# Gated cross attention and a routed expert layer: packed loop counts, a respread closing, smaller GpSimd pieces, and another table of steps

## The reference

```python
h = layernorm(x)
q, k, v = h @ Wq, ctx @ Wk, ctx @ Wv              # 8 heads of 64
o = softmax(q @ k.T / 8) @ v                      # per head, 512 x 1024 scores
x = x + tanh(g_xattn) * (o @ Wo + bo)
h = layernorm(x)
probs = softmax(h @ router.T)                     # 8 experts, each token takes its 2 best
# each expert keeps its CAPACITY (1280) heaviest tokens; kept weights are renormalised per token
y[e] = (h[e] @ W1[e].T * silu(h[e] @ Wg[e].T)) @ W2[e].T   # width 1024 inside
x = x + tanh(g_ffn) * sum over the kept experts of weight * y[e]
```

## Time and profile before

| | |
|---|---|
| median of 3 runs | 1721.95 us (1721.58 to 1724.79) |
| profiled execution | 1727.69 us, its span 1726.0 us |
| TensorE busy | 1642.6 us (95%), clock 0.996 |
| VectorE busy | 1270.0 us (74%) |
| ScalarE, GpSimd busy | 1050.0 us (61%), 671.9 us (39%) |
| chain that ended last | PE 76%, DVE 11%, issue 4%, POOL 3%, ACT 3% |

### The profile page before, as it was taken

The page is one execution under the profiler, slowest core; times in us unless marked ns, Lnnn a source line. Parts: engine busy times, 40 slices in busy tenths (PEclk is TensorE's granted clock), DMA queues, the critical chain, the costliest instruction groups (busy, mean ns, idle before and its releaser), DMA issues.

```text
span 1726.0 us, 33535 instructions
## 1 busy us (share of the span) xinstructions
PE 1642.6 (95%) x12454; PEld 1494.2 (87%) x12454; DVE 1270.0 (74%) x2595; ACT 1050.0 (61%) x2179; POOL 671.9 (39%) x615
## 2 busy tenths in 40 slices
PE   6999999999999999999999998999999999999997
PEld 4788878887888887888888886889999999999997
DVE  6887888888888888888888878676565556547443
ACT  5776766766767666766676766535454455546443
POOL 3342444444345345245345334423343422232322
PEclk9999999999999999999999999999999999999999
DMA  4200220121121021031030022314423421341212
GB/s 126 124 25 1 85 77 26 64 86 38 35 107 45 17 121 50 13 124 51 13 124 32 20 120 85 135 44 106 114 41 108 111 34 39 97 113 28 38 32 28
DMA packets 60555, 115.49 MB, mean 67 GB/s; under 512 B 6616, under 2 KB 48480, under 8 KB 59776
## 3 DMA queue, kind: packets, MB, share of 16 engines
q1 hardware_dynamic: 37104, 79.24, 13.0%
q0 software_dynamic: 15392, 18.66, 5.9%
q10 hardware_dynamic: 7920, 15.73, 2.6%
HBM read 90.27 MB, written 57.42 MB: 86 GB/s over the span
## 4 chain that ended last, share of the span: by engine, by line
PE 76%; DVE 11%; issue 4%; POOL 3%; ACT 3%; DMA 1%; POOLq 0%; DVEq 0%; SPq 0%; ACTq 0%
PE ring L1207 11%; PE turned L1101 11%; PE ffn L1064 10%; PE ffn L1066 10%; PE ffn L1065 10%; PE scores L1089 9%; DVE neg_max L1888 5%; PE ring L1064 4%; PE ring L1066 3%; PE ring L1065 3%; DVE pt_l L1665 2%; PE ring L1173 1%; PE ring L1175 1%; POOL lists L855 1%; POOL probs L889 1%
## 5 line engine op out<-in xcount | busy, mean ns | idle before, releaser
L889 POOL TENSOR_SCALAR probs<-probs,row_rec 128x1024 f32<-128x1024 f32 x254 | 282.2, 1123 | 478.6 <-DVE row_rec L1991 466.9
L1429 ACT ACTIVATE pt_h<-turned 128x512 fp32r<-128x512 f32 x512 | 279.5, 602 | 209.7 <-PE turned L1101 209.2
L1665 DVE TENSOR_TENSOR pt_l<-turned,pt_h 128x512 fp32r<-128x512 f32 x512 | 331.0, 680 | 7.2 <-ACT pt_h L1429 6.8
L1888 DVE TENSOR_REDUCE neg_max<-scores 128x1 f32<-128x1024 f32 x256 | 301.5, 1218 | 35.7 <-PE scores L1089 35.6
L1101 PE MATMUL turned<-ident,probs 128*128 128x128 f32 x2048 | 281.9, 279 | 30.3 <-DVE pt_l L1665 23.3
L1101 PEld LDWEIGHTS turned<-ident,probs 128*128 128x128 f32 x2048 | 224.2, 141 | 98.4 <-issue 69.9
L1485 ACT ACTIVATE probs<-scores,neg_max 128x1024 f32<-128x1024 f32 x256 | 285.3, 1117 | 14.9 <-DVE neg_max L1888 14.8
L1207 PE MATMUL ring<-pt_h,v_hl 128*128 128x256 f32 x1024 | 261.4, 293 | 0.2
L1207 PE MATMUL ring<-pt_l,v_hl 128*128 128x256 f32 x1024 | 250.9, 283 | 0.0
L2256 DVE TENSOR_TENSOR act_f<-ffn,silu 128x256 f32<-128x256 f32 (+1 forms) x232 | 108.4, 467 | 130.7 <-ACT silu L1599 123.3
L1207 PEld LDWEIGHTS ring<-pt_h,v_hl 128*128 128x128 f32 x1024 | 195.7, 191 | 4.0 <-issue 1.9
(11 more groups left out here) (258 smaller groups left out, 3905.4 us busy)
## 6 DMA issues: line engine op xcount, KB each, us to landing
lists<-pads SPq DMA_DIRECT2D x8, 4160.0 KB
w_raw<-w_t ACTq DMA_DIRECT2D x10, 1024.0 KB, 8.3
e_rows<-lists SPq DMA_DIRECT2D x26, 390.0 KB
ctx_raw<-ctx_t SPq DMA_DIRECT2D x15, 512.0 KB, 3.8
wg_raw<-wg_t ACTq DMA_DIRECT2D x5, 1024.0 KB, 7.8
x_in<-x SPq DMA_DIRECT2D x8, 512.0 KB, 4.0
x_sum<-x SPq DMA_DIRECT2D x8, 512.0 KB, 4.0
out<-x_sum SPq DMA_DIRECT2D x8, 512.0 KB, 2.9
```

The costliest lines, as they stand in the source:

```text
L889: nc.gpsimd.tensor_scalar(probs[:, k, :], probs[:, k, :], row_rec[:, k:k + 1], 1.0, ALU.mult, ALU.mult).then_inc(scaled, 1)
L1429: return nc.scalar.activation(dst, src, ACT.Copy)
L1665: return nc.vector.tensor_tensor(dst, src, hi_part.bitcast(F32), ALU.subtract)
L1888: nc.vector.tensor_reduce(neg_max[:, k:k + 1], scores[:, n % 2, :].rearrange("p (a c) -> p a c", a=2), AX.XY, ALU.max, negate=True).then_i ...
```

## The change

1. **Table of steps.** `JOBS` has the same jobs at other steps. The last batch keeps its table, written out. A new table `LOW_EARLY` says for the other batches how many of the two `low_turned` of an even step stand between its two maxima (1 or 2) instead of behind them. SP waits for job q(0,0) instead of v(0,0) before it loads the next x.
2. **GpSimd's pieces.** `split_ctx` makes its copy in two instructions of 128x512 instead of one of 128x1024, and its subtraction in four of 128x256.
3. **Closing.** `chain` has steps 4 to 16 spread otherwise. The table of counts is made in two parts (slots 0 and 1), the search's parts come one slot later or more, and the last one (normalising the kept weights) falls in part c = 1 of the first chunk behind the closing (`search(FC + 1)`).
4. **Loop counts.** VectorE packs each expert's two counts into 6 bits and four experts into a number. TensorE reads two such numbers once, in front of the search loop, and takes the counts of experts 1 to 7 out with shifts and remainders in registers; `before` is carried from expert to expert. The other engines still read theirs.

```diff
 JOBS = {
     0: [("w", 1, 0), ("k", 1, 0)],
     2: [("w", 1, 1)],
     3: [("k", 1, 1)],
     4: [("w", 1, 2), ("q", 1, 0)],
     6: [("w", 1, 3)],
-    7: [("v", 1, 0)],
-    8: [("v", 1, 1), ("k", 2, 0)],
-    10: [("k", 2, 1)],
-    12: [("h", 0, 0), ("v", 1, 2)],
-    13: [("q", 2, 0)],
-    14: [("v", 1, 3)],
-    15: [("q", 3, 0)],
-    16: [("h", 1, 0), ("w", 0, 0)],
-    18: [("w", 0, 1)],
-    19: [("l", 0, 0)],
-    20: [("k", 3, 0), ("w", 0, 2)],
-    21: [("k", 3, 1)],
-    22: [("x", 0, 0), ("x", 1, 0)],
-    23: [("v", 0, 0)],
-    24: [("w", 0, 3), ("k", 0, 0)],
-    27: [("q", 0, 0), ("r", 0, 0)],
-    28: [("k", 0, 1), ("v", 0, 1)],
-    29: [("v", 0, 2)],
+    7: [("k", 2, 0)],
+    8: [("v", 1, 0)],
+    9: [("v", 1, 1)],
+    10: [("q", 2, 0)],
+    12: [("k", 2, 1)],
+    13: [("h", 0, 0)],
+    14: [("v", 1, 2)],
+    15: [("w", 0, 0)],
+    16: [("w", 0, 1), ("k", 3, 0)],
+    17: [("v", 1, 3)],
+    18: [("h", 1, 0)],
+    19: [("w", 0, 2), ("l", 0, 0)],
+    20: [("k", 3, 1), ("q", 3, 0)],
+    22: [("x", 0, 0)],
+    23: [("w", 0, 3), ("x", 1, 0)],
+    24: [("v", 0, 0), ("k", 0, 0)],
+    26: [("k", 0, 1)],
+    27: [("v", 0, 1), ("r", 0, 0)],
+    28: [("v", 0, 2), ("q", 0, 0)],
     30: [("v", 0, 3)],
 }
+LOW_EARLY = {0: 2, 2: 2, 4: 1, 8: 2, 12: 2, 14: 1, 16: 1, 18: 1, 22: 1, 24: 1, 28: 1, 30: 1}
...
-                (0, 0): (4, 5, 6, 7, 8), (0, 1): (9, 10), (0, 2): (11,), (0, 4): (12, 13), (0, 5): (14, 15),
-                (0, 6): (16,), (0, 7): (17, 18), (1, 0): (19,), (1, 1): (20,), (1, 2): (21,), (1, 4): (22, 23),
+                (0, 0): (4, 5, 6, 7), (0, 1): (8, 9), (0, 2): (10, 11), (0, 5): (12, 13), (0, 6): (14, 15),
+                (0, 7): (16,), (1, 0): (17, 18), (1, 1): (19, 20), (1, 2): (21,), (1, 4): (22, 23),
...
-                nc.gpsimd.tensor_scalar(ctx_h[:, :, part], ctx_raw[:, :, :], 1.0, 1.0,
-                                        ALU.mult, ALU.mult).then_inc(ctx_hi, 1)
+                for kc in range(KC):
+                    last = nc.gpsimd.tensor_scalar(ctx_h[:, kc, part], ctx_raw[:, kc, :], 1.0, 1.0,
+                                                   ALU.mult, ALU.mult)
+                last.then_inc(ctx_hi, 1)
...
-                nc.gpsimd.tensor_tensor(ctx_l[:, :, part], ctx_raw[:, :, :],
-                                        ctx_h[:, :, part].bitcast(F32), ALU.subtract)\
-                    .then_inc(ctx_split, 1)
+                for kc in range(KC):
+                    for keys in range(2):
+                        raw = slice(keys * (M // 4), (keys + 1) * (M // 4))
+                        cols = slice(part.start + raw.start, part.start + raw.stop)
+                        last = nc.gpsimd.tensor_tensor(ctx_l[:, kc, cols], ctx_raw[:, kc, raw],
+                                                       ctx_h[:, kc, cols].bitcast(F32), ALU.subtract)
+                last.then_inc(ctx_split, 1)
...
@@ TensorE @@
-                part = {1: 1, 4: 3, 6: 4, 8: 5}.get(slot)
+                part = {1: 1, 5: 3, 6: 4, 9: 5}.get(slot)
...
+                    for k in range(2):
+                        loops.append(pe.value_load(table[0:1, 3, 3 + k:4 + k], min_val=1,
+                                                   max_val=(1 << FIELD * PER_WORD) - 1))
...
-                wides = pe.value_load(table[0:1, 4, ds(e, 1)], min_val=1, max_val=2)
-                chunks = pe.value_load(table[0:1, 0, ds(e, 1)], min_val=1, max_val=T // CHUNK)
-                before = pe.value_load(table[0:1, 1, ds(e, 1)], min_val=0, max_val=MOST_CHUNKS)
+                both = loops[(e - 1) // PER_WORD] >> FIELD * ((e - 1) % PER_WORD)
+                wides = pe.snap(both % 4)
+                chunks = pe.snap((both >> 2) % (1 << FIELD - 2))
...
@@ VectorE @@
+                    done = 0
+                    if body.own and (body.prev or u >= 2):
+                        done = (LAST_EARLY if body is LAST else LOW_EARLY).get(u, 0)
...
-                        if lows:
-                            low_turned(b, u - 2, 0)
-                            low_turned(b, u - 2, 1)
+                        for j in range(done):
+                            low_turned(b, u - 2, j)
...
-                part = {0: 0, 1: 1, 3: 2, 4: 3, 6: 4, 8: 6}.get(slot)
+                part = {0: 0, 1: 7, 2: 1, 3: 2, 4: 3, 8: 4, 9: 6}.get(slot)
...
+                    own(nc.vector.scalar_tensor_tensor(table_f[:, 7, :], table_f[:, 0, :], 4.0,
+                                                       table_f[:, 4, :], ALU.mult, ALU.add))
+                    v.wait_ge(search_seq, 24)
+                    v.wait_ge(powers, PER_WORD)
+                    own(nc.vector.tensor_tensor(table_f[:, 7, 1:E], table_f[:, 7, 1:E], table_f[:, 8, 1:E], ALU.mult))
+                    v.wait_ge(search_seq, 25)
+                    own(nc.vector.reduce_sum(table_f[:, 2, 2:3], table_f[:, 7, 1:1 + PER_WORD], AX.X))
+                    own(nc.vector.reduce_sum(table_f[:, 2, 3:4], table_f[:, 7, 1 + PER_WORD:E], AX.X))
...
+                    nc.vector.tensor_copy(table[:, 3, 3:5], table_f[:, 2, 2:4])
```

More of the change, by code:

```diff
@@ L71 @@
 TWICE = [[2 * n, 2 * n + 1] for n in range(PIECES // 2)]
-FILL_A = 32
+FILL_A = 16
 WIDE_PIECES = [[0, 1], [2, 3], [4, 5], [6, 7], [8, 9], [10], [11]]
 LAG = 4
-TABLED = 23
+TABLED = 27
+FIELD = 6
+PER_WORD = 4
 RW = D + 4
 JOBS = {
+    0: [("w", 1, 0), ("k", 1, 0)],
+    2: [("w", 1, 1)],
+    3: [("k", 1, 1)],
+    4: [("w", 1, 2), ("q", 1, 0)],
+    6: [("w", 1, 3)],
+    7: [("k", 2, 0)],
[17 more added lines that the diff above has]
+    28: [("v", 0, 2), ("q", 0, 0)],
+    30: [("v", 0, 3)],
+}
+START_JOBS = [("x", 0, 0), ("x", 1, 0), ("k", 0, 0), ("q", 0, 0), ("k", 0, 1)]
+FIRST_VALUES = {0: [("v", 0, 0), ("v", 0, 1)], 1: [("v", 0, 2)], 2: [("v", 0, 3)]}
+LOW_EARLY = {0: 2, 2: 2, 4: 1, 8: 2, 12: 2, 14: 1, 16: 1, 18: 1, 22: 1, 24: 1, 28: 1, 30: 1}
+LN_STEPS = 6
+GATE_STEPS = 27
+RANK_STEPS = 5
+CONSTS = 16
+NEXT_FROM = 22
+SLOT_OF = {job: u for u, jobs in JOBS.items() for job in jobs}
+END_STEPS = 27
+END_JOBS = {0: [("w", 1, 0)], 2: [("w", 1, 1)], 4: [("w", 1, 2)], 6: [("w", 1, 3)],
+            12: [("h", 0, 0)], 14: [("h", 1, 0)], 16: [("l", 0, 0)], 22: [("r", 0, 0)]}
+LAST_JOBS = {
     0: [("w", 1, 0), ("k", 1, 0)],
@@ L127 @@
 SECOND_LOWS = [10, 11]
-LOW_BETWEEN = (24, 26, 28, 30)
+LAST_EARLY = {24: 2, 26: 2, 28: 2, 30: 2, UNITS - 1: 2}
 class Body:
@@ L1339, in chunk @@
                         down(g, c - BEHIND, parity)
+                    if c == 1 and isinstance(n, int):
+                        search(FC + 1)
                 for c in range(FC - BEHIND, FC - 1):
@@ L1415, in expert @@
                     whole_chunk(pe.snap(before + wides + j), parity, ST)
+                return pe.snap(before + wides + chunks)
             chunk(0, 0, True)
-            first_expert()
+            before = first_expert()
             for e in range(1, E):
-                expert(e, e % 2)
+                before = expert(e, e % 2, before)
         @block.scalar
@@ L1960, in step @@
                     jobs = body.results(u)
-                    lows = body is LAST and u in LOW_BETWEEN + (UNITS - 1,)
-                    late = [(what, c) for what, c in jobs if lows and what[0] == "r"]
+                    done = 0
+                    if body.own and (body.prev or u >= 2):
+                        done = (LAST_EARLY if body is LAST else LOW_EARLY).get(u, 0)
+                    late = [(what, c) for what, c in jobs if body is LAST and done and what[0] == "r"]
                     jobs = [job for job in jobs if job not in late]
@@ L1995, in step @@
                     between(body, u, 2)
-                    if (body.prev if u < 2 else body.own) and not lows:
+                    if (body.prev if u < 2 else body.own) and done < 1:
                         low_turned(b, u - 2, 0)
-                        between(body, u, 3)
+                    between(body, u, 3)
+                    if (body.prev if u < 2 else body.own) and done < 2:
                         low_turned(b, u - 2, 1)
-                    else:
-                        between(body, u, 3)
                     between(body, u, 4)
@@ L2236, in chunk @@
                             finish(n - 1, v.snap((n - 1) * ST), ST)
+                    if c == 1 and follows and e == 0:
+                        search(FC + 1)
                     if c == 4:
@@ L2289, in _ @@
             nc.vector.memset(e_base[:, :], 0.0).then_inc(base_done, 1)
+            for k in range(PER_WORD):
+                nc.vector.memset(table_f[:, 8, 1 + k:E:PER_WORD], float(1 << FIELD * k)).then_inc(powers, 1)
             closing(step, rows_of, early, nothing, nothing, search)
```

29 lines of the change are left out of this document (12 added, 17 removed).

## The result

| | before | after |
|---|---|---|
| median of the runs | 1723.11 us | 1728.95 us |
| spread | 1721.58 to 1724.79 (6 runs) | 1727.74 to 1730.41 (6 runs) |
| profiled execution, its own time | 1727.69 us | 1728.71 us |
| its span | 1726.0 us | 1727.0 us |

The ratio is 1.0027, 95% interval 1.0017 to 1.0038: slower, and the interval leaves out 1. The two profiled executions differ by only 1 us, because that of before lay 4.6 us above its own median and that of after at its median. That difference turns out to matter.

What follows compares the result with a forecast made beforehand. The prediction took TensorE to bound the kernel, busy 128.84 of 132 us in a full batch. Gains of 5 + 4 + 3 + 3 + 6.5 = 21.5 us took the median from 1721.95 to 1700 us, range 1687 to 1713.

Steps and rivals of the forecast that it cites:

- pieces: GpSimd's context subtraction in four pieces shortens its blocks of VectorE's routing product: 5 us gained, bounds 0 and 6.
- table, six batches: Moved jobs and early pt_l in the full batches cut TensorE's waits: 4 us gained, bounds -10 and +12.
- table, batch 0: The same table in batch 0 cuts its 5.8 us of waits for pt_l: 3 us gained, bounds 0 and +6.
- closing: Respread closing steps and later search cut TensorE's waits for rows, act_f and the search product: 3 us, bounds -2 and +6.
- counts: At experts' starts, TensorE's idle goes without its loads of counts: 6.5 us gained, bounds 0 and +8.2.
- Three batches at 2.0 us are 6.0 us: Blocks of VectorE's routing product by GpSimd's subtraction lengthen three of six full batches by 2.0 us each.
- second bound: For GpSimd's pieces: if VectorE is held once by each of the four, the gain is near 0 instead of 6 us.
- The 0.8 us for w(0,2) in step 19: New wait in each full batch: w(0,2) reads the last o of step 18 with only h and T between.
- 0.7 for register arithmetic: In the experts, 0.7 us taken off the counts' gain for working out counts in TensorE's registers.
- (a): The table gives nothing or costs a little, new waits in steps 12 to 19 eating its gain: 1707 us; chance 0.17.
- (b): At experts' starts ScalarE's and VectorE's own loads are just behind; 5 us return as silu waits: 1705 us; chance 0.12.
- (d): In the batches, the second maximum's delay makes scores wait for exponentials, 0.45 us a step: 1734 us; chance 0.06.

Runs made afterwards that it cites:

- r first: Kernel before with the new table alone, and in step 27 the product r put ahead of projection v(0,1): 1720.2 us, ratio 0.9957.
- p_table: Kernel before with only the new table of steps, its early pt_l orders and SP's wait: 1725.8 us, ratio 0.9990.
- held registers: Each expert's three loop values moved once into registers: kernel before with packed counts alone 1720.3 us, ratio 0.9960; whole changed kernel 1723.6 us, ratio 0.9984.
- p_pieces: Kernel before with only GpSimd's smaller pieces (two copies, four subtractions a half): 1729.4 us, ratio 1.0012.
- held counts: Kernel before with the packed counts alone, their three values per expert moved once into registers: 1720.3 us, ratio 0.9960.
- closing_r_later: Kernel before with the new closing alone, and in it the product that ranks the last batch's tokens one part later: 1728.5 us, ratio 1.0001.
- the run of the counts: Kernel before with only the packed loop counts, in the old closing, values not held in registers: 1728.1 us, ratio 1.0008.

## Why the prediction was wrong

Point by point, the term of the sum against what the runs had:

| step of the prediction | predicted | measured |
|---|---|---|
| pieces | -5 us | +2 (0 to +4) alone |
| table, six batches | -4 us | +1.8 us in the profile (795.0 for 793.3); -2 with r first |
| table, batch 0 | -3 us | -2.1, and -3.1 in p_table |
| closing | -3 us | +1 (-1 to +3) |
| counts | -6.5 us | +1.4 (-0.3 to +3); -6.9 with held registers |

**Pieces.** The block itself was read rightly: 1.97 us for 0.19, released with the end of GpSimd's subtraction. The step that failed is "Three batches at 2.0 us are 6.0 us": it took one execution for all. Three other executions with this table and whole subtractions have no block. And p_pieces, where no block of 2 us is left and the six batches cost 1.7 us more (795.0 for 793.3), came out at +2 us (0 to +4), so the executions that it is compared with can have had about one block on the mean, not three. The page's execution stood 5.7 us above the median of the runs then known, about the size of three blocks, and the prediction used that only as an offset. That it was the blocks is not shown: on the chips of the experiments the median of the kernel before is 1725.5 to 1727.7 us, about what that execution took. The prediction also saw only the subtraction. What puts the product into it is the copy ahead of it, and the cut of the copy, for which it gave no reason, is what lets the next product through; the two cuts were not run apart. The second bound was priced too low too: "near 0 if that happens". The Trainium skill's rule ("SBUF — State Buffer", Who interferes with whom: whoever issues first holds the shared ports for the whole instruction, and issue order decides who blocks) agrees with the race at the copy: 0.18 us for a product that starts 0.02 us ahead of it, 1.09 for one that starts with it. What I did not count is that pieces end later, 2.8 and 3.4 us for 2.4, and that in the first half the end is what met the product.

**Table.** The part that said waits at x(1,0), and in steps 16 and 26, would go was right, 8.0 us of ot_x and most of the old pt_l row. The new waits were put in the wrong places. The 0.8 us for w(0,2) in step 19 do not show in the profile. In their place are step 0 (1.3 us) and step 23 (1.7 us, 1.3 with whole subtractions), with 0.4 us more in step 12, behind GpSimd's scaling. For step 0 the sentence that failed is the one of the other moved steps, that they come 10 us or more before their use: r was not in that list at all. It had kept its step number, 27, but the table took one projection out of steps 28 to 30, so TensorE reached the next batch 1.45 us sooner while eight scatters and a landing of 2.4 us took what they always take. For step 23 the cover was counted against the first half of pt_l ("the jobs need last only 1.0 us"), and the second half, which the value 1 in the table leaves behind the maximum, was not counted.

**Closing.** +1.0 (rows) and +1.1 (the search product: 1.7 us left, 1.9 predicted) were right. Moving the logits one part later and leaving the ranks where they were cost 1.9 us at chosen, and act_l 0.9. A stall that is taken out by moving a step later is paid for by the next consumer of that step, and I had named only the step.

**Counts.** "The loads are the cost, and all of it can go" was right: without the loads, and with held counts, 8.2 us of idle are down to 0.2. "0.7 for register arithmetic" is the term that failed. It was priced as if it ran once an expert, but it ran at each loop turn and grew with the expert, and it cost 8.4 us. Right in its kind was that silu is late next, 1.6 us for 1 predicted.

**Rivals.** None was it. (a) named the table, and was right in that, (b) and (d) did not happen: the waits for exponentials did not grow in the six batches. What made the kernel slower are two terms that came out with the wrong sign. Against executions of the old table without blocks the changed kernel loses 3.7 us in the six batches (797.0 for 793.3) and 3.3 us in the experts (521.8 for 518.5), and wins back 2.1 to 2.7 us in batch 0; that is 4 to 5 us in profiled executions, and 0.27% is 4.7. The larger single cause is the register arithmetic: held registers alone turn +0.27% into -0.16%. With r first as well the kernel is 0.4% faster, and with the pieces and the new closing left out 0.9%.

## What to carry to other kernels

A value that a loop uses should be moved into a register once; look at what the queue executes per turn, since an expression costs again wherever its name stands, and idle that has no releaser at loop turns is its sign. Before a stall of a few profiled batches is booked as a gain, look for it in a second execution of the same code, all the more where the profiled one is slower than the median of the runs. And follow a blocked instruction back: what was late may have been held by another instruction before. When steps of a table are moved, follow the chains of fixed length that start in it (scatters, landings, a scaling behind them) to the one who waits at their end: taking work from behind the head of such a chain has the same effect as starting it later.

## What the runs showed of the hardware

A margin of some 0.02 us decides between two states of a batch. In five executions with the old table and whole subtractions, the 25 products that start 0.003 to 0.07 us ahead of GpSimd's copy take 0.18 us, and their batches 131.9 to 132.5. The five that start between 0.003 us ahead of it and 0.018 us behind take 1.08 to 1.09, the next product 1.96 to 1.97, and the batch 134 us or more. An execution can have none, two or three of these.

Runs of one kernel differ by 3 us (the changed kernel) to 12 us (23 runs of the kernel before on one chip) at the same work, and the clock accounts for part of it. The granted clock over the span was 0.996 in those executions of the held counts that took 1716.6 and 1718.8 us, and 0.992 in that of 1722.2. In the kernel before it is 1.00 over the full batches (195 to 990 us) and over the experts (1200 to 1700 us). It is lower where the last batch leaves TensorE idle; the stretches of the kernel before and of the changed kernel (length, busy time and count of each engine, clock, DMA share, GB/s):

```profile
1060.00:1090.00 30.00, 23.38 (x166) 20.67 (x165) 22.25 (x47) 19.53 (x38) 19.07 (x18) 0.89 0.31 115
```

```profile
1060.00:1090.00 30.00, 23.44 (x165) 20.94 (x166) 21.02 (x51) 19.41 (x37) 22.38 (x21) 0.89 0.35 124
```

TensorE had waited 1.7 us for exponentials and 2.6 us for the scaling in this stretch, and part of it ran at 1.2 in place of 2.4 GHz. In the held counts and in closing_r_later the same stretch had 0.94, in the run of the counts 1.00. From GpSimd's last normalisation to expert 1 the profiled executions take 197 to 204 us, also where the code there is the same. A change of less than 0.2% can't be told from this by one execution.
